# Contracting all 128 rows of the projected block in the step-size products of a two-way Mamba and mixture-of-experts layer

## The reference, cut to what matters

```python
def _mamba_dir(xz, conv_w, conv_b, xproj_w, dtproj_w, dt_bias, A_log, Dp):
    x, z = (xz[:, :d_inner], xz[:, d_inner:])
    u = _causal_conv_silu(x, conv_w, conv_b)
    x_dbl = jnp.einsum('bdl,kd->bkl', u, xproj_w)               # 8 + 16 + 16 rows
    delta = jnp.einsum('dr,brl->bdl', dtproj_w, x_dbl[:, :r])   # r = 8
    Bm, Cm = x_dbl[:, r:r + n], x_dbl[:, r + n:]
    delta = jax.nn.softplus(delta + dt_bias[None, :, None])
    dA = jnp.exp(jnp.einsum('bdl,dn->bdln', delta, -jnp.exp(A_log)))
    dBx = jnp.einsum('bdl,bnl,bdl->bdln', delta, Bm, u)
    h = _ssm_scan(dA, dBx)
    y = jnp.einsum('bdln,bnl->bdl', h, Cm) + Dp[None, :, None] * u
    return y * jax.nn.silu(z)
```

## Time and profile before

| | |
|---|---|
| median of 3 runs | 1097.3 us (1092.97 to 1101.39) |
| the profiled execution, span | 1105.0 us |
| mean granted PE clock | 0.938 |
| PE busy | 932.6 us (84%) |
| DVE busy | 1030.1 us (93%) |
| ACT busy | 940.6 us (85%) |
| POOL busy | 909.1 us (82%) |
| L1176, 64 records | 36.5 us |
| L1160, 64 records | 48.8 us |
| L1185, 64 records | 31.6 us |

### The profile page before, as it was taken

How to read it: one execution, slowest core, us unless ns; L and a number is a source line. 1 busy time by engine, 2 the same in 40 slices (tenths; PEclk the granted TensorE clock), 3 DMA queues, 4 the chain that set the end, 5 groups by cost and what they waited for, 6 DMA issues and landing times.

```text
span 1105.0 us, 21807 instructions
## 1 busy us (share of the span) xinstructions
PE 932.6 (84%) x5794; PEld 735.3 (67%) x5866; DVE 1030.1 (93%) x1361; ACT 940.6 (85%) x1755; POOL 909.1 (82%) x567
## 2 busy tenths in 40 slices
PE   4569889955789898999998989989889989988894
PEld 2133333324678787878887877878778878877783
DVE  7789999777999999999999999999999999988897
ACT  3247999968899989999998999999989989988960
POOL 4178888863679999999999899989999999989762
PEclk9778888677999999999999999999999999998997
DMA  9945655689556767687778767776876787666668
GB/s 306 371 147 204 249 197 187 254 282 309 169 166 172 215 193 212 175 238 195 187 201 212 203 166 211 195 208 174 233 200 178 210 216 203 161 171 164 174 137 240
DMA packets 153108, 228.87 MB, mean 207 GB/s; under 512 B 36301, under 2 KB 98029, under 8 KB 147701
## 3 DMA queue, kind: packets, MB, share of 16 engines
q1 hardware_dynamic: 125844, 208.39, 58.6%
q0 software_dynamic: 27136, 19.02, 12.3%
HBM read 161.84 MB, written 69.64 MB: 209 GB/s over the span
## 4 chain that ended last, share of the span: by engine, by line
POOL 34%; issue 30%; ACT 14%; PE 10%; DVE 6%; DMA 3%; SPq 2%; POOLq 1%; ACTq 0%; DVEq 0%; another core or an unknown queue 0%
POOL arena L838 19%; POOL acc_d L823 14%; ACT arena L1068 3%; PE ps L1176 2%; PE ps L1160 2%; ACT arena L986 1%; DMA acc_d<-yrows,tags 1%; PE ps L1145 1%; ACT arena L1007 1%; DVE arena L1464 1%; ACT arena L937 1%; ACT arena L933 1%; ACT arena L1036 1%; PE ps L1244 1%; PE ps L1273 1%
## 5 line engine op out<-in xcount | busy, mean ns | idle before, releaser
L1568 DVE TENSOR_TENSOR_SCAN arena<-arena,ps 128x512 f32<-128x512 f32 x512 | 599.0, 1205 | 1.8 <-issue 0.8
L838 POOL TENSOR_TENSOR arena<-arena 128x1024 f32<-128x1024 f32 x246 | 527.2, 2469 | 54.6 <-DVE arena L1568 34.9
L1068 ACT ACTIVATE arena<-delta,a_neg 128x511 f32<-128x511 f32 x512 | 341.3, 728 | 2.6 <-DVE arena L1568 2.4
L823 POOL DMA_INDIRECT acc_d<-yrows,tags x160 | 252.7, 1579 | 45.2 <-issue 37.1
L1244 PE MATMUL ps<-ident,arena 128*128 128x128 f32 x2048 | 270.2, 275 | 4.6 <-DVE arena L1576 3.4
L1556 DVE TENSOR_TENSOR ps<-du,ps 128x512 f32<-128x512 f32 x352 | 233.2, 679 | 25.9 <-issue 9.5
L1244 PEld LDWEIGHTS ps<-ident,arena 128*128 128x128 f32 x2048 | 232.9, 142 | 15.1 <-DVE arena L1576 3.8
L804 POOL DMA_INDIRECT slots_d<-arena,pos x128 | 149.2, 1165 | 40.2 <-issue 35.8
L1273 PE MATMUL ps<-w,arena 128*128 128x128 f32 x1248 | 173.9, 282 | 3.4 <-ACT arena L1036 3.0
L1273 PEld LDWEIGHTS ps<-w,arena 128*128 128x128 f32 x1248 | 153.7, 192 | 12.8 <-issue 3.8
L1265 PE MATMUL ps<-rowsT,w 128*128 128x256 f32 x640 | 154.7, 385 | 7.8 <-ACT arena L1018 7.5
(11 more groups left out here) (154 smaller groups left out, 915.2 us busy)
## 6 DMA issues: line engine op xcount, KB each, us to landing
arena<-c_d SPq DMA_DIRECT2D x128, 512.0 KB
w<-w_dram SPq DMA_DIRECT2D x80, 258.0 KB
w<-w_dram SPq DMA_DIRECT2D x80, 256.0 KB
rows<-slots_d SPq DMA_DIRECT2D x80, 130.0 KB
slots_d<-delta SPq DMA_DIRECT2D x5, 2015.0 KB, 18.7
delta_d<-arena SPq DMA_DIRECT2D x8, 1024.0 KB
du_d<-delta SPq DMA_DIRECT2D x8, 1024.0 KB
delta<-delta_d SPq DMA_DIRECT2D x8, 1024.0 KB, 6.6
```

Of the source, the lines that this page charges most:

```text
L823: pool.indirect_dma_start(acc_d[j % W_RING], bass.IndirectOffsetOnAxis(ap=tags[:, j, a, 0:1].bitcast(I32), axis=0), yrows[:, j % W_RING, a ...
L838: nc.gpsimd.tensor_tensor(state[:, q % H_RING], state[:, q % H_RING], c_rows[:, r % C_RING], ALU.mult).then_inc(s["prod_done"], 1)
L1068: nc.scalar.activation(decay[:, q % DA_RING, j, lo:lo + L - 1], delta[:, par, dh, lo:lo + L - 1], ACT.Exp, scale=a_neg[:, dh, 2 * g + j:2 ...
L1568: nc.vector.tensor_tensor_scan(state[:, q % H_RING, j, way], decay[:, q % DA_RING, j, way], b_ps[:, ROW[q, j], j, way], 0.0, ALU.mult, ALU ...
```

## The change

The four matmuls of a pass now contract all 128 partitions: weights `dtw[:, d, ...]` against `xdbl[:, d, :]`. So that the 119 other rows add nothing, `dtw` is set to zero once by DVE, at the very start of its program, and SP waits for that before it issues the loads of weights, two of which write rows 96 to 104 of `dtw`.

```diff
@@ in block.sync
                 if k == 0:
                     sp.dma_start(route[:, 0:3 * E], route_in).then_inc(s["route_in"], 16)
+            sp.wait_ge(s["dtw_zero"], 1)
             for dst, src in ((chan[:, :, :], chan_in), (inw, inw_in), (xproj, xproj_in), (dtw[BR:BR + NR], dtw_in),
@@ in block.tensor, prepare(b)
                     for h in range(NH):
-                        last = nc.tensor.matmul(ps[:, DT_BANK + d * NH + h, :], dtw[BR:BR + NR + 1, d, h * P:(h + 1) * P],
-                                                xdbl[BR:BR + NR + 1, d, :], start=True, stop=True)
+                        last = nc.tensor.matmul(ps[:, DT_BANK + d * NH + h, :], dtw[:, d, h * P:(h + 1) * P],
+                                                xdbl[:, d, :], start=True, stop=True)
@@ in block.vector
+            nc.vector.memset(dtw, 0.0).then_inc(s["dtw_zero"], 1)
             dve.wait_ge(s["consts_in"], 16)
             nc.vector.tensor_copy(ident[:, :], consts[:, C_ID:C_ID + P])
```

More of the change, by code:

```diff
@@ L461, in build_kernel @@
         m_ps = [ps[:, 6, :], ps[:, 7, :]]
-        names = """consts_in route_in wts_in a_exp zero_v zero_acc slots_zeroed var_ready std_ready xn_ready xnT_ps xnT_ready
+        names = """consts_in route_in wts_in dtw_zero a_exp zero_v zero_acc slots_zeroed var_ready std_ready xn_ready xnT_ps xnT_ready
             kw_ready bias_ready behind_ready experts_ready xn_act_ready shift_ready score_ps score_ready sel_ready logit_ps keys_ps chosen_ready rank_ps pos_ready gdiff_ready gexp_ready
```

## The result

| | before | changed |
|---|---|---|
| median | 1097.6 us (15 runs, 1092.97 to 1101.44) | 1102.8 us (15 runs, 1097.35 to 1107.97) |
| ratio to before, 95% interval | | 1.0049 (1.0034 to 1.0064) |
| profiled span | 1105.0 us | 1105.0 us |
| mean granted PE clock | 0.938 | 0.951 |
| PE, ACT, DVE busy | 932.6, 940.6, 1030.1 us | 921.2, 939.8, 1031.9 us |

The changed kernel is 0.49% slower, 5.4 us (3.7 to 7.0) on 1097.6. The forecast was 3.7 us slower, and a time within 1% of before as the likeliest.

A forecast was written before the change was run, and what follows sets the result against it. DVE was taken to bound passes 1 to 5, ACT with PE from pass 6. Three cold passes gave +2.9 us, four +4.5; the middle, +3.7 on 1097.3, gave 1101.0 us, range 1091.0 to 1106.5.

The forecast's parts named there:

- Memset and SP's wait cost nothing: At the start, the DVE memset takes 0.5 to 0.9 us, covered before SP's held-back transfer at 6.16 us; cost nothing.
- The clock stays up behind the burst: Behind the step-size matmuls, `L1160` runs at 592 ns; saves PE 3.1 us in pass 3, 1.5 in pass 2.
- Rival 2: Clock does not follow rows in use, or zero-weight rows count as nothing; only 0.3 us of PE moves, 1097.3 us; chance 0.12.
- Worth nothing in the passes 1 to 5: PE time saved in these passes gains nothing, since DVE is full there and does not wait.
- The gap grows to 3.5 or 3.6 us and the clock falls: PE's idle time before the second `L1167` grows from 0.39 or 2.08 us; three or four cold passes, chance 0.50.
- Rival 1: The clock holds in the longer gap, so only the 1.7 us of pass 6 count: 1095.6 us; chance 0.28.
- The price of a cold `project_x`, 1.61 us: ACT waits 2.77 us for `L1145` instead of 1.16 in each cold pass, at most 6.4 us over passes 1 to 4.
- ACT's slack of 2.2 us: ACT's lead over DVE by pass 5 covers part of ACT's loss for DVE, but does not help in pass 6.
- The 0.26 us, 1.17 and 0.51 us that come off in pass 6: ACT's pass 5 wait for DVE (0.26) and pass 6 waits for `L1176` (1.17) and `L1160` (0.51) are subtracted.
- four-cold case: `L1145` cold in all of passes 1 to 4: 4 x 1.61 - 0.26 - 1.17 - 0.51 = +4.5 us.
- The first rows of C move with DVE's `L1491`: SP's transfers behind pass 6 start later with DVE's `L1489`, some 4 us; at most 0.5 us absorbed, left out.
- Rival 3: Freed PE time lets ACT and DVE run closer everywhere, at most 12.3 us: 1085 us; chance 0.03.

The follow-up runs named there:

- e2_zero_only: The kernel before with the zeroing of `dtw` and SP's wait for it, but matmuls of nine rows; ratio 0.9998 to before.
- e3_rows32: The changed kernel with the step-size matmuls contracted over 32 partitions (rows 96 to 127) instead of 128; ratio 1.0006 to before.
- e1_fill: The changed kernel with the four skip products of each pass issued twice, the second time writing the same values; ratio 1.0007 to before.
- e5_half_skip: The kernel before, nine rows, with half of the skip products of each pass left out; ratio 1.0046 to before.
- e8: The kernel of e1_fill with two of the four scatters of each token left out; ratio 0.9978 to before.
- e10: The kernel of e1_fill with SP's four reads of gate and skip for batch 0 issued behind the first rows of C; ratio 0.9995 to before.
- e11_after_late: The changed kernel with SP's four reads of gate and skip for batch 0 issued behind the first rows of C; ratio 1.0023 to before.
- e9_before_late: The kernel before with SP's four reads of gate and skip for batch 0 issued behind the first rows of C; ratio 0.9980 to before.
- e6_half_fill: The changed kernel with half of the skip products issued twice; ratio 1.0009 to before.

## Why the prediction was right

- **The matmuls themselves**: 592 ns for 588, no cost. Right.
- **Memset and SP's wait cost nothing**: right (e2_zero_only, 0.9998).
- **The clock stays up behind the burst**: right. 592 ns in `L1161`, 1.00 in both windows. One reading behind it was wrong: the idle time of 0.39 us lies behind the stretch of pass 3, not ahead of it. Ahead of it PE had been idle for 2.08 us, with warm records in between. But the 0.39 us stand ahead of the burst of pass 4, and `L1160` was cold there too, 6.53 us for eight records, so the conclusion holds. Rival 2 falls, and e3_rows32 adds that the rows in use count, also where their weights are zero, and that 32 of them are not enough.
- **Busy time as the measure**: by the Trainium skill, "TensorE: Matmul & The Clock Gate", "Part 1: The HAM clock gate", the clock follows how busy the engine is. It was busy for all of both windows at nine rows with the clock at 0.89 and 0.50, and for all of both at 128 rows with 1.00. The measurement decides: busy time does not tell it.
- **Worth nothing in the passes 1 to 5**: right, the preparation of e1_fill and of e3_rows32, one with the warm and one with the cold `L1161`, is 122.8 and 122.7 us. That DVE waits for nobody from pass 1 on was not quite so: before had one wait of 0.82 us in pass 1.
- **The gap grows to 3.5 or 3.6 us and the clock falls**: right, 3.66 us in each, and all four passes were cold, where I took the middle of three and four. Rival 1 falls. e5_half_skip shows that the gap alone is enough, e1_fill that without it the loss is gone. The Trainium skill, in the section "Why this matters for your kernels" of the same page, warns of idle gaps between bursts; these rows agree. What the prediction overlooked is that its own cold `project_x` of pass 0 stood behind a gap of 1.57 us, shorter than the 2.55 us that it took as harmless. The length of the last gap alone was too simple a test, and it gave the right answer because the new gaps were far longer.
- **The price of a cold `project_x`, 1.61 us**: slightly low. ACT's waits were 2.96, 2.65, 2.96 and 2.78 for 1.16, so 1.80, 1.49, 1.80 and 1.62. Pass 0 gave 0.19 more. In sum 6.9 us, where four cold ones had been put at 6.4.
- **ACT's slack of 2.2 us covers DVE for a part**: right. DVE's `L1483` waits for ACT from pass 2 on, 1.19, 0.89, 1.16 and 0.73 us.
- **The 0.26 us, 1.17 and 0.51 us that come off in pass 6**: this step failed at its end. They came off: from pass 0 to `L1491` of pass 6 the changed kernel takes 222.95 - 81.83 = 141.1 us, before took 221.66 - 84.30 = 137.4, so 3.8 us more, where some 4 were forecast. (With the measured 6.9 us the sum would be 6.9 - 0.26 - 1.68 = 5.0. Of the difference, 0.8 us is that pass 0, cold in both, was that much shorter in the changed kernel.) But what e1, e8 and e10 show is that the 1.68 us of waits do not carry to the end. Without them the four-cold case would have been 6.44 - 0.26 = 6.2 us, and both this and my own four-cold value of 4.5 lie inside the interval of the measured 5.4 us (3.7 to 7.0). So the timed runs of the changed kernel alone don't show this step wrong; the filled kernels do.
- **The first rows of C move with DVE's `L1491`, and the end with them**: right for the changed kernel, where they start 175.3 us behind pass 0 against 170.6 in e2_zero_only. But they are not what carries the loss, as far as one pair shows it: in e11_after_late they move by 0.6 us against e9_before_late and the kernel loses 4.7. And a gain of 1.7 us moves them by 1.1 us or by nothing, and the end by nothing that was measured.
- **Rival 3, a real gain**: no. With the clock up but for one `project_x` and hardly a gap (e1_fill) the kernel is where it was. Its price counted eight waits of ACT for `L1145`; there are five.

So the mechanism was right, and 3.7 us lies at the edge of the measured interval. Both of its errors, three or four cold passes for four and 1.7 us for nothing, made the forecast too small; neither hid the other.

## What to carry to other kernels

Speeding up a burst on an engine that is not the bound only moves its idle time, and on TensorE that idle time can cost the clock for the next burst, the one that somebody waits for: look at the gap that the saved time will make, and at who waits behind it. Count the path's slack first, since it decides how many such losses show. And do not count time that is gained at the end of a stage until a run shows it at the end of the kernel: here a loss of 5 us came through, and a gain of 1.7 us did not in any of three pairs.

## What the runs showed of the hardware that I had not expected

- Work taken away made the kernel slower (half of the skip products gone: 1.0046), and work that nobody needs made it no slower than before (the skip products twice: 1.0007, against 1.0049 without).
- A burst over 32 rows costs the clock like one over nine: medians of 1009 and 1061 ns for the line behind, against 592 with 128 rows, of which 119 have zero weights.
- Short gaps can cost the clock as well: four records behind 1.20 us idle took 3.48 us (e1_fill) and behind 1.57 us 3.59 (before), instead of 1.99. One gap of 2.36 us cost the clock, and one of 2.38 in the same kernel did not (e6_half_fill). All 17 gaps of 3.4 us or more did.
